# A batch's state built one step after its closing, the tile chain ten steps behind, one set of token rows: a decoder layer with 8 experts on one core

## What is computed

```python
q = softmax(x @ Wq.T + bq over a head's 16 channels); k = softmax(x @ Wk.T + bk over the 1024 tokens)
state = einsum('bhnd,bhne->bhde', k, v)            # one state per batch and head
out = layernorm(einsum('bhnd,bhde->bhne', q, state)) @ Wo.T + bo
x = layernorm(x + out)
x = layernorm(x + softmax(q k' + mask) v')          # 77 context keys per batch, 8 heads
w = top 4 of 8 of softmax(x @ router_w), renormed   # experts 256 -> 1024 -> 256, gelu
x = layernorm(x + sum_e w_e * (gelu(x @ up_w[e]) @ down_w[e]))
```

## Time and profile before

| | |
|---|---|
| median of 3 runs | 1258.03 us (1257.5 to 1259.54) |
| the profiled execution's own time | 1262.06 us |
| its span | 1260.1 us |
| PE busy | 1086.4 us (86%) |
| DVE busy | 764.3 us (61%) |
| POOL busy | 647.3 us (51%) |
| ACT busy | 495.3 us (39%) |
| HBM read and written | 51.91 MB and 36.04 MB, 70 GB/s over the span |

### The profile page before, as it was taken

The page is one execution under the profiler, slowest core; times in us unless marked ns, Lnnn a source line. Parts: engine busy times, 40 slices in busy tenths (PEclk is TensorE's granted clock), DMA queues, the critical chain, the costliest instruction groups (busy, mean ns, idle before and its releaser), DMA issues.

```text
span 1260.1 us, 27063 instructions
## 1 busy us (share of the span) xinstructions
PE 1086.4 (86%) x8572; PEld 908.3 (72%) x8572; DVE 764.3 (61%) x1863; ACT 495.3 (39%) x913; POOL 647.3 (51%) x738
## 2 busy tenths in 40 slices
PE   6668877878886699988899999999999999999960
PEld 3345665656565588877788888888888888888750
DVE  1667988977797687765744444444444444444325
ACT  3754533544353255543233333333333333333214
POOL 3013327745673777766775465555555555554424
PEclk9779989988897799999999999999999999999995
DMA  5431223222212233334444654465544445553325
GB/s 163 150 105 60 93 85 93 77 78 63 76 38 64 67 60 74 73 63 75 60 72 79 131 89 78 77 77 77 77 77 77 77 77 77 77 77 60 65 55 242
DMA packets 163039, 105.07 MB, mean 83 GB/s; under 512 B 107596, under 2 KB 153856, under 8 KB 162656
## 3 DMA queue, kind: packets, MB, share of 16 engines
q1 hardware_dynamic: 132896, 67.67, 21.2%
q0 software_dynamic: 30016, 35.68, 19.7%
HBM read 51.91 MB, written 36.04 MB: 70 GB/s over the span
## 4 chain that ended last, share of the span: by engine, by line
PE 59%; DVE 17%; POOL 11%; issue 6%; ACT 3%; DMA 3%; SPq 0%; POOLq 0%; DVEq 0%; ACTq 0%
PE big L1665 25%; PE big L1684 13%; PE trans L1684 12%; POOL slot_records L781 3%; POOL rstd L757 3%; PE big L1707 2%; DVE stat L1049 2%; PE small L1753 2%; POOL early_sums L811 2%; POOL ve L755 1%; DVE w_up L1045 1%; PE small L1585 1%; PE big L1709 1%; DVE w_down L1045 1%; DVE pr L1334 1%
## 5 line engine op out<-in xcount | busy, mean ns | idle before, releaser
L1665 PE MATMUL big<-xgT,w_up 128*128 128x256 f16 (+1 forms) x3456 | 408.5, 267 | 14.4 <-DMA xgT<-xg 11.7
L1665 PEld LDWEIGHTS big<-xgT,w_up 128*128 x3456 | 325.3, 98 | 57.8 <-issue 18.3
L904 ACT ACTIVATE h<-big,up_scale 128x512 f32<-128x512 f32 x270 | 185.5, 687 | 449.9 <-PE big L1665 436.8
L1298 DVE TENSOR_SCALAR hh<-h,h_scale 128x512 f16<-128x512 f32 x270 | 133.5, 494 | 314.0 <-ACT h L904 312.2
L811 POOL DMA_INDIRECT token_sums<-y,rec x99 | 164.2, 1659 | 243.0 <-ACT y L912 205.9
L1684 PE MATMUL big<-w_down,hh 128*128 x1264 | 217.8, 274 | 2.7 <-DVE hl L1300 2.4
L1300 DVE SCALAR_TENSOR_TENSOR hl<-h,h_scale,hh 128x512 f16<-128x512 f32 x270 | 203.0, 752 | 9.6
L1684 PE MATMUL big<-w_down,hl 128*128 x632 | 173.4, 274 | 0.0
L1684 PE MATMUL trans<-w_down,hh 128*128 x896 | 153.4, 273 | 2.5 <-DVE hl L1300 2.4
L781 POOL DMA_INDIRECT slot_records<-recs,posi x128 | 130.0, 1015 | 35.6 <-issue 33.6
L1684 PEld LDWEIGHTS big<-w_down,hh 128*128 128x128 f16 x1264 | 124.2, 98 | 21.5 <-issue 5.2
(11 more groups left out here) (251 smaller groups left out, 1511.9 us busy)
## 6 DMA issues: line engine op xcount, KB each, us to landing
w_down<-in_L_ffn_up_w_dram SPq DMA_DIRECT2D x8, 1024.0 KB, 5.1
w_down<-in_L_ffn_down_w_dram SPq DMA_DIRECT2D x7, 1024.0 KB, 6.0
XA<-in_x_dram SPq DMA_DIRECT2D x32, 128.0 KB, 2.8
XRES<-in_x_dram SPq DMA_DIRECT2D x32, 128.0 KB, 2.6
token_rows<-XR SPq DMA_DIRECT2D x32, 128.0 KB, 1.9
sums<-token_sums SPq DMA_DIRECT2D x8, 512.0 KB, 6.5
out_dram<-sums SPq DMA_DIRECT2D x8, 512.0 KB, 2.6
xgT<-xg SPq DMA_TRANSPOSE x135
```

Of the source, the lines that this page charges most:

```text
L904: act.activation(h[:, i % H_RING, :], psu[up_bank(i)], ACT.Gelu_apprx_tanh, scale=k["up_scale"][:, t:t + 1]).then_inc(gelu_ready, 1)
L1298: dve.tensor_scalar(hh[:, i % HALF_RING, :], h[:, i % H_RING, :], k["h_scale"][:, t:t + 1], None, ALU.mult).then_inc(hh_ready, 1)
L1665: ins = pe.matmul(psu[up_bank(i)][:, j * size(t):(j + 1) * size(t)], w[:, ws, c, m:m + P], xgT[:, t % 2, xs * CC + c, 0:size(t)], start=(n ...
```

## The change

- `chain_tile` starts one step later (`TB + 2`). A closing step now has a c0, for the last tile of the batch before; the step behind it has the next batch's first projection and no c0.
- The state is built in the step behind the closing (`state_built`). Since tiles of the next batch arrive meanwhile, the first two tiles of a batch have homes that alternate, with one extra tile for keys and values in a part of the up weights' memory that is filled later. Q has nine tiles. The subtraction and the exponentials of the keys go in five groups in place of four.
- `PIECE_STEPS` is other, `HALF_STEPS` are 18 and 21 in place of 16 and 20. The last piece is loaded into the memory of `wqkv` and `XA` as soon as the last projection is done, squared in step 35 and split in step 36.
- `key_blocks` and its transposes stand at the end of a step (10, 19, 28, 37) in place of its start.
- `load_values` stands in the third step behind the closing, in place of the second: steps 11, 20, 29, 38.
- `rows1`, `acc1`, `slots1` and their copies are gone; the early tiles gather from and add to the first 2048 rows of `rows` and `acc`.
- `STEPS` = 50, `EARLY` = 19, `MIX0` stays 38, so `MIXED` = 12.

```diff
-PIECE_STEPS = [2, 3, 4, 5, 6, 7, 8, 9, 12, 15, 18, 21, 24, 28, 32, 36]
-HALF_STEPS = [TB + 4 + HT * (half + 1) for half in range(HALVES)]
+PIECE_STEPS = [2, 3, 4, 5, 6, 7, 8, 9, 11, 13, 15, 19, 23, 28, 32, 35]
+HALF_STEPS = [2 * TB + 2, 2 * TB + 5]
-EARLY = 18
+EARLY = 19
-MIX0 = PIECE_STEPS[-1] + 2
+MIX0 = PIECE_STEPS[-1] + 3
 def chain_tile(s, d):
-    return first_tile(s - (TB + 1) - d)
+    return first_tile(s - (TB + 2) - d)
+def state_built(s):
+    return closing(s - 1) if s >= 1 else None
+EXTRA = TB
+HOME = [[0, 1], [EXTRA, 1], [0, EXTRA], [1, 0]]
+KEY_GROUPS = [(0, 1), (1, 2), (2, 4), (4, 6), (6, 8)]
...
-            return V[:, :, :, :].rearrange("p t c m -> p (t c m)")[:, 0:CC * HID]
+            return first_stage[:, 0:CC * HID]
...
-                    sp.wait_ge(sm_ready, SM["st", B - 1, CC - 1] + 1)
+                    sp.wait_ge(big_ready, BIG["qkv", NT - 1] + 1)
                     sp.wait_ge(w_split, n)
...
-                if g < EARLY_TILES:
-                    sp.dma_start(rows1_out[g], XR[:, g % 2, :].bitcast(F32)).then_inc(rows_stored[g % 2], 16)
...
-                    sp.wait_ge(records_copied, 16 * EXP)
+                    for half in range(HALVES):
+                        sp.wait_ge(scattered[half], 16 * HT * TOPK * EARLY_BATCHES)
...
-                if i == 2 and 0 <= b < B:
+                if i == 3 and 0 <= b < B:
                     load_values(b)
...
-                    for g in range(EARLY_TILES):
-                        sp.dma_start(acc_out[g], acc1_out[g]).then_inc(sums_copied, 16)
...
-                if close is not None:
-                    build_state(close)
+                if state_built(s) is not None:
+                    build_state(state_built(s))
...
-                    if a >= TB:
-                        act.wait_ge(sm_ready, SM["st", a // TB - 1, CC - 1] + 1)
+                    if home_before(a) is not None:
+                        act.wait_ge(sm_ready, SM["st", home_before(a), CC - 1] + 1)
```

More of the change, by code:

```diff
@@ L59 @@
 HT = TB // HALVES
-KG = 4
 EXPONENT = 0x7F800000
@@ L106, in closing, with home, home_before @@
     return b if b < B and i == TB else None
+def state_built(s):
+    return closing(s - 1) if s >= 1 else None
+EXTRA = TB
+HOME = [[0, 1], [EXTRA, 1], [0, EXTRA], [1, 0]]
+def home(g):
+    b, i = divmod(g, TB)
+    return HOME[b][i] if i < 2 else i
+def home_before(g):
+    return max((u // TB for u in range(g) if home(u) == home(g)), default=None)
+KEY_GROUPS = [(0, 1), (1, 2), (2, 4), (4, 6), (6, 8)]
 def square_piece(s):
@@ L134, in rows_moved @@
 def rows_moved(g):
-    return sum(32 if u < EARLY_TILES else 16 for u in range(g % 2, g + 1, 2))
+    return 16 * (g // 2 + 1)
 def bank_uses():
@@ L192, in bank_uses @@
             use(sm, "rt", c4)
-        if closing(s) is not None:
+        if state_built(s) is not None:
             for c in range(CC):
-                use(sm, "st", closing(s), c)
+                use(sm, "st", state_built(s), c)
         for half in range(HALVES):
@@ L201, in bank_uses @@
             use(sm, "early")
+        b, i = divmod(s - TB - 2, TB + 1)
+        if i == 0 and 0 <= b < B:
+            for c in range(CC):
+                use(sm, "kt", b, c)
     use(sm, "cnt")
@@ L218, in big_places @@
     return place, before, held
-MIXED_TILE = chain_tile(MIX0, 2)
+MIXED_TILE = min(chain_tile(s, 2) for s in range(MIX0, MIX0 + 2) if chain_tile(s, 2) is not None)
 BIG_PLACE, BIG_BEFORE, BIG_LAST = big_places()
@@ L306, in layer_kernel, with layer @@
             k[name] = keep(name, shape, dt)
[L307 to L310 removed]
+        layer(nc, k, rows, acc, slots, x, ctx, mask, Wq, bq, Wk, bk, Wv, bv, Wo, bo, ln_g, ln_b, xb, router, up, down, out)
+def layer(nc, k, rows, acc, slots, x, ctx, mask, Wq, bq, Wk, bk, Wv, bv, Wo, bo, ln_g, ln_b, xb, router, up, down, out):
     st, places = ExitStack(), ExitStack()
@@ L649, in _ @@
                     load_piece(2 * EXP - 1)
-                if s == record_step(EARLY_BATCHES) - 1:
-                    for half in range(HALVES):
-                        sp.wait_ge(scattered[half], 16 * HT * TOPK * EARLY_BATCHES)
-                    for e in range(EXP):
-                        at = slice(e * CAP, e * CAP + EARLY_BATCHES * N)
-                        sp.dma_start(slots1[at, :], slots[at, :]).then_inc(records_copied, 16)
                 if s == MIX0 - 2:
@@ L1381, in _ @@
                 close = closing(s)
-                b, i = divmod(s - TB - 2, TB + 1)
-                if i == 0 and 0 <= b < B:
-                    key_blocks(b)
                 if s == TB:
@@ L1445, in _ @@
                     second_sum(c3)
+                b, i = divmod(s - TB - 2, TB + 1)
+                if i == 0 and 0 <= b < B:
+                    key_blocks(b)
                 if s == 0:
@@ L1758, in _ @@
                     pe.matmul(small_into(("early",))[:, 0:EXP], ones[:, :], counted[:, :, 0], start=True, stop=True).then_inc(sm_ready, 1)
+                b, i = divmod(s - TB - 2, TB + 1)
+                if i == 0 and 0 <= b < B:
+                    pe.wait_ge(ctx_loaded, 16 * (b + 1))
+                    for c in range(CC):
+                        pe.transpose(small_into(("kt", b, c))[:, 0:KEYS], ctx_sb[:, c * P:(c + 1) * P], ident[0:KEYS, 0:KEYS]).then_inc(sm_ready, 1)
             for s in range(MIX0, STEPS):
```

106 lines of the change are left out of this document (51 added, 55 removed).

## The result

The changed kernel is slower: median 1270.3 us in the first measurement and 1269.7 in a second one of five runs, against 1258.7 and 1258.6 for the kernel before. The ratios are 1.0086 (1.0068 to 1.0103) and 1.0098 (1.0082 to 1.0114). One execution of the first measurement took 1307.0 us at a granted clock of 0.863, a slower state, and is in no ratio. The forecast was 1252.4, faster, with a range up to 1261.

What follows compares the result with a forecast made beforehand. DVE's work and waits were taken to bound the kernel ahead of the mix, PE from there. Mix start -12.8, stages +4.5, value loads +5.6, last norms -3.0: -5.7 us from 1262.06, median 1252.4; range 1246 to 1261.

Steps and rivals of the forecast that it cites:

- DVE's work up to step 37: Ahead of step 37: four chain stages, `gates` and `key_blocks` leave, the last piece's split comes in; -5.4 us.
- chain stages moved into the mix: In the mix: four more chain stages run on PE, at about 1.3 us each; +4.5 us, from 4.0 to 5.1.
- SP's value loads in step 38: In step 38: value loads ahead of the second expert tile's turned rows make PE wait 6.3 us; +5.6 us, between 0 and 7.
- waits for the last norm: Late in the mix: one of two steps behind eight scatters on POOL has no c4 left to wait; -3.0 us.
- DVE's waits: Ahead of step 37: state waits stay 20.4 us; first closing -3.0, `key_blocks` transposes -2.5, step 36 +1.2 us.
- Step 36: Step 36 splits a piece squared late in step 35, without projection work on DVE as cover; +1.2 us, between 0 and 1.5.
- `key_blocks`: Steps 19 and 28: its transposes no longer hold back the projection, `gates` lies over them; -2.5 us, between 0 and 2.7.
- The clock: Projections behind the closings, steps 18 and 27, may run at half clock; +2.3 us, from 0 to 4.5 for each.
- The third rival: Each projection at half clock costs up to 4.5 us; from the third further one the kernel is slower, 1263.5; chance 0.19.
- The first closing: First batch's closing: the wait for the exponentials goes, 2.46 us of PE, and tile 8's projection runs beside DVE; -3.0 us.
- The hand-over: From step 37 to the first up product: gather starts at 2.8 us, up product 9.5 later, 12.3 for 17.7; -5.4 us.
- Hidden things: Second stores, copied records, the sums' copy and POOL's wait for it lie beside PE's work; they cost or give nothing.

Runs made afterwards that it cites:

- again: The changed kernel run once more, unchanged, for a profile; 1269.74 us, its profiled execution 1264.73 us.
- again_two: The changed kernel run once more, unchanged, for a second profile; its profiled execution took 1270.06 us.
- values_behind: The changed kernel with SP's value loads of the last batch in step 38 behind the second expert tile's turned rows; 1259.04 us, ratio 1.0014.
- scatter_alone: The changed kernel with the eight scatters of batch 3's first half in steps 48 and 49 instead of 47 and 48; 1262.96 us, ratio 1.0024.
- before_scatter: The kernel before with the two steps of eight scatters on POOL moved from 45 and 46 to 47 and 48; 1248.49 us, ratio 0.9931.
- late_square: late_norm with `build_state` behind DVE's other work, ACT's last square moved into step 36 and that step's `split_low` behind `choose`; 1251.78 us, ratio 0.9934.
- piece_alone: The kernel before with the last weight piece loaded a step earlier, squared in step 35 and split in step 36; 1260.38 us, ratio 1.0030.
- scatter_late: values_behind with `build_state` behind DVE's other work and the eight scatters of batch 3's first half one step later; 1246.89 us, ratio 0.9904.
- one_set_alone: The kernel before without `rows1`, `acc1`, `slots1` and their copies; 1256.27 us, ratio 0.9987.
- late_norm: values_behind with the last weight piece's norm, `scale` and `split_high` behind stage c4 in step 36 alone; 1259.76 us, ratio 1.0016.

## Why the prediction was wrong

The terms of the sum, and what the profiles gave. Ahead of the mix the changed program is seen in four executions (again, again_two, values_behind, scatter_alone), that of before in two (before, before_scatter):

| term | forecast | measured |
|---|---|---|
| DVE's work up to step 37 | -5.4 | -5.2 |
| DVE's time without work up to step 37 | -2.0 | +7.9 |
| step 37 to the first up product | -5.4 | -5.3 |
| chain stages moved into the mix | +4.5 | +3.0 |
| SP's value loads in step 38 | +5.6 | +7.8 |
| waits for the last norm | -3.0 | 0 to +1.6 |
| sum | -5.7 | +8 to +10 |

The medians differ by 11.1 to 11.6, so 1 to 3 us more than the terms. The two profiled executions of before took 4.0 and 2.4 us longer than the medians of their kernels, the four of the change between 5.0 less and 0.9 more, so the profiles may show too small a difference; they are too few to settle it.

**The step that failed is "DVE's waits"** and with it "step 37 starts 7.4 us earlier". DVE's work was counted rightly: 303.99 to 304.67 us busy against 309.49 and 309.59. But step 37 starts 388.5 to 393.2 us behind the first projection, where it was 386.6 and 389.9. DVE stood 84.3 to 89.3 us in place of 77.1 and 80.3. Its waits up to step 37, from the same profiles (us; idle time with no known releaser left out):

| DVE waits for | before | changed |
|---|---|---|
| projections | 26.5 and 23.5 | 25.7 to 28.8 |
| the state's matmuls | 20.4 and 20.5 | 15.1 to 18.4 |
| c2's logits | 1.6 | 3.9 to 4.1 |
| c1's product | none | 2.9 to 3.3 |
| a weight piece's norm | 1.2 and 0.8 | 1.9 to 2.7 |
| `gates`' sums (`posx`) | none | 0.8 to 1.4 |
| all waits listed | 73.2 and 69.9 | 76.5 to 82.4 |

In the means that is 5.0 more in step 36, 2.2 for projections, 1.9 for c1 in other steps (26 and 35 above all), 1.2 for the sums, 0.9 in small ones, and 3.3 less for the state: 7.9. The prediction had four terms:

- *Step 36, forecast +1.2, measured +5.0.* I priced the late square as the cover that `take_qkv` no longer gives. DVE waited 1.45 + 1.31 + 2.23 us, as the rows of step 36 show. I had asked what waits for the square, not what is queued behind it on ACT: the copy for c1. But that is 2.4 us by late_square, 3.1 stay without it, behind c1 and c2 that ran at half clock in part, which the term did not hold at all. piece_alone has the same square and none of these waits.
- *`key_blocks`, forecast -2.5, nothing won.* The waits of 1.2 and 1.3 us for the projections of steps 19 and 28 went, and 1.6 to 2.0 and 1.4 to 1.7 came back in steps 20 and 29. There the transposes stand ahead of the projection again, and the projection itself took 2.7 to 3.3 us in place of 1.88. How much is due to which isn't separated.
- *The clock, forecast +2.3 for steps 18 and 27.* The third rival's sign was seen: a projection behind a closing took 3.62 us at half clock in again_two, and DVE waited 3.54 and 1.51 us in steps 18 and 27. In `again` it was 0.34 and 1.48. So the term was 1.8 to 5.1, in the range. It named too few places, though. Of the 24 projections of steps 9 to 34, five took over 2.5 us in either profile of before, and seven or eight in those of the change: also those of steps 9 (no wait at DVE), 20 and 29. Step 29's took 3.62 and 3.10 us before, for which DVE waited 4.32 and 2.69; that is now 1.4 to 1.7. In steps 11 and 12 DVE waits 5.1 and 5.5 us in the first two profiles of the change, where steps 10 to 12 had 4.6 and 4.8, with no transpose of the context right ahead; three of these four projections took 3.0 to 3.6 us. The Trainium skill ("TensorE: Matmul & The Clock Gate", What's actually happening) has activity release the throttle. The trace agrees as to the places, behind steps in which PE is seldom busy, but not in each execution: ahead of step 18's projection PE was busy 12.63 of 17.39 us in `again_two`, where it then ran at half clock, and 11.46 of 16.58 in `again`, where it ran at full.
- *The first closing, forecast -3.0.* Its waits for the state fell from 4.6 to 3.5 us; what of the rest belongs to it, the profiles don't separate. Over all four closings these waits are 15.1 to 18.4 us in place of 20.5, so the drop was about as large as forecast, and elsewhere.

**The hand-over was right**, and step by step: the gather 2.9 us behind step 37's start (forecast 2.8), then 9.3 us to the up product (9.5). What stands right ahead of the gather in again_two is c0's deviation on POOL (until 414.6 us), and not the records (issued at 412.2, landed some 2.0 us later); the two lie close together. piece_alone shows the price in DVE's work, paid in step 36.

**SP's value loads: right mechanism, a term too small.** The wait was 6.42 for 6.3 us. What I left at the edge of the range is the half clock behind it (an up group of 2.74 us in place of 1.48): the rest shrank by 7.8 us when the wait went, and the median by 10.7.

**The stages** are 3.0 us of PE's work for four: 772.61 us busy in scatter_late's rest, 769.62 in before_scatter's. A mean over 38 stages is too dear for these four.

**The last norms.** One wait fell from 3.56 us to 1.05, the other grew from 2.98 to 4.88: 0.6 us less in all, for a forecast of 3.0. Priced by the rest, the scatters' place cost 7.0 us before and 7.1 to 8.5 after; by the medians 9.3 before and 6.5 to 6.8 after. The two ways differ by up to 4 us, so this term stays open.

**Hidden things.** The second stores and copies were put at nothing; one_set_alone gained 2.3 us at the median, 0.3 to 3.1 by the ratio. The range missed since its upper end took one mechanism at a time: the waits (+9.9 off) and SP's block (+2.2) came together.

What isn't settled: why some executions of the changed kernel have the half clock in steps 16 to 19 and others not. No run was made that removes it, so what the half clock costs ahead of the mix is read from rows and not from a run without it.

## What to carry to other kernels

When an instruction becomes late, list what stands behind it in its own engine's queue, here a copy behind a square, and not only who waits for its result: moving the waiter (late_norm) gained nothing, moving the late one (late_square) took 2.4 us off the waits. A wait for another engine's long work is gone only if other work is put over it; moving the whole step kept 15.1 to 18.4 of 20.4 us, and moving `build_state` behind `split_low` and `choose` in the same step gained 5.6. Price a wait of TensorE in a stretch that it rules at more than its length; here it was 1.1 to 1.7 times.

## What the runs showed of the hardware

A wait of 6.42 us on TensorE cost 7.8 us in the profiles, one of 4.88 us 7.1 to 8.5, and two of 3.56 and 2.98 us together 7.0. The up group behind the first took 2.74 us in place of 1.48, and the granted clock was 0.59 over the 8 us around the second. Identical programs reached step 37 at 388.5 or 392.9 us, with one projection at full or half clock (1.88 or 3.62 us). And the second gather's issue took 0.95 us with no DVE split beside it, in the changed kernel and in piece_alone; it was 2.83 beside the split. The Trainium skill ("SBUF — State Buffer", Who interferes with whom) lets one expect this, since the split reads two inputs from SBUF, and the trace agrees.
